# Two of four units of a layer's last step: transposed in blocks on VectorE and moved through DRAM instead of on TensorE

## The reference

```python
for layer in (1, 2):
    h = layer_norm(x)                                  # scale and offset
    q, k, v = h @ wq + bq, ctx @ wk + bk, ctx @ wv + bv  # 16 heads of 128
    k, v = append(k, bias_k), append(v, bias_v)        # one learned key and value
    w = softmax(q @ k.T / sqrt(128))
    x = x + (w @ v) @ wo + bo
h = layer_norm(x)
x = x + gelu(h @ w_fc1 + b_fc1) @ w_fc2 + b_fc2
```

## Time and profile before

| | us |
|---|---|
| median of 3 runs | 495.98 |
| lowest, highest run | 494.83, 497.55 |
| profiled execution, its own time | 495.7 |
| its span in the trace | 493.9 |
| layer 0's last step, first score | 205.08 |
| layer 1's last step, first score | 434.04 |

### The profile page before, as it was taken

How to read it: one execution, slowest core, us unless ns; L and a number is a source line. 1 busy time by engine, 2 the same in 40 slices (tenths; PEclk the granted TensorE clock), 3 DMA queues, 4 the chain that set the end, 5 groups by cost and what they waited for, 6 DMA issues and landing times.

```text
span 493.9 us, 11020 instructions
## 1 busy us (share of the span) xinstructions
PE 487.9 (99%) x3216; PEld 442.2 (90%) x3216; DVE 389.8 (79%) x910; ACT 331.3 (67%) x728; POOL 413.9 (84%) x385
## 2 busy tenths in 40 slices
PE   8999999999999999999999999999999999999997
PEld 6789888999999898999988889989989989999997
DVE  4888878878877878857789878778788888766796
ACT  4777767666766866665486777758666677768542
POOL 4977989989898998996597989989989898999561
PEclk9999999999999999999999999999999999999999
DMA  7536777756567676612115786676766566650011
GB/s 240 182 107 199 247 238 211 209 188 193 176 208 195 210 215 191 198 40 66 42 44 172 237 252 183 209 205 195 229 188 196 186 200 185 194 169 1 15 32 42
DMA packets 53159, 82.56 MB, mean 167 GB/s; under 512 B 5904, under 2 KB 33936, under 8 KB 53136
## 3 DMA queue, kind: packets, MB, share of 16 engines
q1 hardware_dynamic: 53136, 82.28, 54.8%
HBM read 53.42 MB, written 28.84 MB: 167 GB/s over the span
## 4 chain that ended last, share of the span: by engine, by line
PE 90%; DMA 3%; DVE 3%; POOL 1%; SPq 1%; issue 1%; ACT 1%; ACTq 0%; DVEq 0%; POOLq 0%
PE ring L1224 67%; PE ps_ctx L1224 10%; PE acc L1224 10%; DMA spill<-blocks 1%; PE ring L1270 1%; DMA all_cols<-cols_in 1%; DMA wf_lo<-spill 1%; SPq L287 1%; DVE pT_lo L922 0%; PE ring L1307 0%; DVE h_lo L1003 0%; POOL rstd L412 0%; ACT q_hi L598 0%; DVE blocks L900 0%; POOL wf_lo L370 0%
## 5 line engine op out<-in xcount | busy, mean ns | idle before, releaser
L937 DVE TENSOR_REDUCE row_max<-ring 128x1 f32<-128x512 f32 x112 | 76.1, 688 | 27.6 <-PE ring L1224 27.3
L661 ACT ACTIVATE probs<-ring,shift 128x512 f32<-128x512 f32 x112 | 76.5, 684 | 18.7 <-DVE shift L942 18.6
L432 POOL TENSOR_TENSOR v_lo<-v_sum,v_hi 128x512 fp32r<-128x512 f32 x64 | 83.0, 1299 | 3.0 <-ACT v_hi L611 3.0
L900 DVE STREAM_TRANSPOSE blocks<-probs 128x512 f32<-128x512 f32 x108 | 70.1, 687 | 5.6 <-POOL probs L439 5.4
L439 POOL TENSOR_SCALAR probs<-probs,inv 128x512 f32<-128x512 f32 x80 | 55.5, 701 | 20.3 <-DVE inv L950 20.2
L444 POOL TENSOR_TENSOR pT_lo<-wf_lo,pT_hi 128x1024 fp32r<-128x1024 f32 x28 | 67.1, 2418 | 0.0
L1224 PE MATMUL ring<-pT_lo,v_hi 128*128 128x256 f32 x208 | 58.5, 281 | 0.2 <-DVE pT_lo L922 0.2
L1224 PE MATMUL ring<-pT_hi,v_lo 128*128 128x256 f32 x208 | 58.0, 279 | 0.0
L1224 PE MATMUL ring<-pT_hi,v_hi 128*128 128x256 f32 x208 | 58.0, 279 | 0.0
L593 ACT ACTIVATE k_hi<-ring,cols 128x512 fp32r<-128x512 f32 x57 | 37.7, 689 | 30.1 <-PE ring L1224 30.0
L1224 PE MATMUL ring<-wv_lo,cT_hi 128*128 128x256 f32 x200 | 55.9, 279 | 0.0
(11 more groups left out here) (215 smaller groups left out, 1634.6 us busy)
## 6 DMA issues: line engine op xcount, KB each, us to landing
spill<-blocks SPq DMA_DIRECT2D x54, 512.0 KB, 2.9
wf_lo<-spill SPq DMA_DIRECT2D x112, 128.0 KB, 3.3
wf_hi<-spill SPq DMA_DIRECT2D x104, 128.0 KB, 3.1
wk_raw<-wk_in SPq DMA_DIRECT2D x17, 256.0 KB, 2.7
wq_raw<-wq_in SPq DMA_DIRECT2D x17, 256.0 KB, 3.7
wv_raw<-wv_in SPq DMA_DIRECT2D x16, 256.0 KB, 3.9
vrows<-vrows_in SPq DMA_DIRECT2D x16, 256.0 KB, 4.1
wo_raw<-wo_in SPq DMA_DIRECT2D x16, 256.0 KB, 2.7
```

The costliest lines, as they stand in the source:

```text
L432: pool.tensor_tensor(v_lo[:, 2 * m:2 * m + 2, :], v_sum[:, m % 2, :].rearrange("p (t c) -> p t c", c=PW), v_hi[:, 2 * m:2 * m + 2, :].bitc ...
L661: act.activation(probs[:, u, q, :], ring[S_BANKS[where][QTB * u + q]][:], ACT.Exp, bias=shift[:, u, q:q + 1], scale=SCALE, accum_out=row_s ...
L900: last = dve.transpose(blocks[:, u % 2, :, :, q, :].rearrange("p g c b -> p c g b"), probs[:, u, q, :].rearrange("p (c g b) -> p c g b", g ...
L937: dve.reduce_max(row_max[:, u, q:q + 1], ring[S_BANKS[where][QTB * u + q]][:], AX_X).then_inc(max_done, 1)
```

## The change

In `last_step` the units 0 and 1 go the way of the steady steps: `transpose_blocks` on VectorE, `write_blocks` and `read_blocks` on SP, `round_moved` on ScalarE, `moved_rest` on VectorE. Only units 2 and 3 are transposed on TensorE: `transpose_own` 0 to 3 are now what 4 to 7 were (`NT` is 4 instead of 8). The orders of all engines in `last_step` are changed with it. Since the steady machinery now runs in every step for units 0 and 1, the semaphore counts lose their `- layer` (`pair - layer` becomes `pair`), and SP adds by hand, for units 2 and 3 of a last step, what their moves would have added.

Cut to its core (left out: the renamed counts in the helpers):

```diff
-NT = NU * 2
+NT = 4
-PT_BANKS = [3, 1, 4, 0, 3, 0, 5, 0]
+PT_BANKS = [3, 0, 5, 0]
...
@@ SP @@
-            def last_step(pair, final=False):
+            def last_step(pair, layer, final=False):
+                sp.wait_ge(wo_split, pair)
+                load_wo(pair)
+                for u in range(2):
+                    write_blocks(pair, layer, u, False)
+                for u in range(2):
+                    read_blocks(pair, layer, u, False)
+                for u in range(2, NU):
+
+                    sp.wait_ge(landed[u], QB * LOAD * pair)
+                    sp.sem_inc(blocks_ready, 1)
+                    sp.sem_inc(landed[u], QB * LOAD)
+                    sp.sem_inc(spilled[u], LOAD)
                 if not final:
                     sp.wait_ge(wk_split, pair + 2)
                     load_wk(pair + 2)
-                sp.wait_ge(wo_split, pair)
-                load_wo(pair)
-                if not final:
                     sp.wait_ge(wo_split, pair + 1)
                     load_wo(pair + 1)
...
@@ GpSimd, last_step @@
                 split_wo(pair - 1)
-                residual(layer, 0)
-                normalise(pair, 0, [0])
+                normalise(pair, 0, [0, 1])
+                normalise(pair, 1, [1])
                 moved_rest(pair - 1, layer, 2)
                 value_rest(pair, 0)
                 moved_rest(pair - 1, layer, 3)
-                normalise(pair, 0, [1])
-                normalise(pair, 1, [1])
+                normalise(pair, 2, [0, 1])
                 value_rest(pair, 1)
                 pool.wait_ge(k_filled, NK * (pair + 1))
                 split_wk(pair + 1)
-                normalise(pair, 2, [0, 1])
-                residual(layer, 1)
+                residual(layer, 0)
+                value_rest(pair, 2)
                 pool.wait_ge(outputs_done, layer + 1)
                 split_wo(pair)
-                value_rest(pair, 2)
                 value_rest(pair, 3)
+                residual(layer, 1)
                 inverse_deviation(layer + 1, 0)
...
@@ ScalarE @@
             def exponential(pair, u, q, where, layer, first=False):
-                if not first:
-                    act.wait_ge(blocks_ready, NU * (pair - 1 - layer) + u + 1)
+                if not first or layer > 0:
+                    act.wait_ge(blocks_ready, NU * (pair - 1) + u + 1)
...
@@ ScalarE, last_step @@
                 exponential(pair, 1, 1, "last", layer)
                 round_v(pair, 0, layer)
+                normalise(pair, 1, [0])
                 round_moved(pair - 1, layer, 3)
                 round_o(pair - 1, 1, "last")
                 exponential(pair, 2, 0, "last", layer)
                 round_v(pair, 1, layer)
                 exponential(pair, 2, 1, "last", layer)
-                normalise(pair, 1, [0])
                 round_o(pair - 1, 2, "last")
                 exponential(pair, 3, 0, "last", layer)
-                round_o(pair - 1, 3, "last")
-                round_own(pair, layer, 0)
-                round_own(pair, layer, 1)
-                round_own(pair, layer, 2)
                 exponential(pair, 3, 1, "last", layer)
                 round_v(pair, 2, layer)
-                round_own(pair, layer, 3)
-                normalise(pair, 3, [0])
+                normalise(pair, 3, [0, 1])
+                round_o(pair - 1, 3, "last")
+                round_moved(pair, layer, 0)
+                if final:
+                    act.activation(table_load[:], dim_cols[:, 0:1], ACT.Gelu)
+                round_moved(pair, layer, 1)
+                round_v(pair, 3, layer)
                 if not final:
                     round_k(pair + 1, 0, "last")
-                else:
-                    act.activation(table_load[:], dim_cols[:, 0:1], ACT.Gelu)
-                round_v(pair, 3, layer)
-                normalise(pair, 3, [1])
                 round_o(pair, 0, "own")
                 round_o(pair, 1, "own")
-                round_own(pair, layer, 4)
-                round_own(pair, layer, 5)
-                round_own(pair, layer, 6)
-                round_own(pair, layer, 7)
+                for j in range(NT):
+                    round_own(pair, layer, j)
...
@@ VectorE, last_step @@
                 maximum(pair, 1, 0, "last")
-                split_o(pair - 1, 0, "last")
                 shifts(pair, 1, 0)
                 maximum(pair, 1, 1, "last")
+                shifts(pair, 1, 1)
+                inverse_sums(pair, 0)
+                split_o(pair - 1, 0, "last")
                 dve.wait_ge(wv_split, pair + 1)
                 sum_v(pair, 0, "last")
-                inverse_sums(pair, 0)
-                shifts(pair, 1, 1)
+                inverse_sums(pair, 1)
+                transpose_blocks(pair, layer, 0)
+                transpose_blocks(pair, layer, 1)
                 maximum(pair, 2, 0, "last")
+                shifts(pair, 2, 0)
                 sum_v(pair, 1, "last")
-                shifts(pair, 2, 0)
                 maximum(pair, 2, 1, "last")
                 shifts(pair, 2, 1)
-                inverse_sums(pair, 1)
                 split_o(pair - 1, 1, "last")
                 maximum(pair, 3, 0, "last")
                 shifts(pair, 3, 0)
                 maximum(pair, 3, 1, "last")
                 shifts(pair, 3, 1)
+                inverse_sums(pair, 2)
                 split_o(pair - 1, 2, "last")
                 sum_v(pair, 2, "last")
-                split_own(pair, layer, 0)
-                split_own(pair, layer, 1)
-                inverse_sums(pair, 2)
+                inverse_sums(pair, 3)
                 split_o(pair - 1, 3, "last")
-                split_own(pair, layer, 2)
-                inverse_sums(pair, 3)
+                moved_rest(pair, layer, 0)
                 sum_v(pair, 3, "last")
-                split_own(pair, layer, 3)
+                moved_rest(pair, layer, 1)
                 split_o(pair, 0, "own")
...
@@ TensorE, last_step @@
                 pe.wait_ge(v_summed, NV * pair + 2)
                 context(2, "last")
                 unit_output(0)
                 pe.wait_ge(o_split, NU * (pair - 1) + 2)
                 project_v(2, "last")
-                pe.wait_ge(pT_split[3], done)
+                pe.wait_ge(pT_split[3], pair)
                 pe.wait_ge(exp_done, NS * pair + 5)
                 context(3, "last")
+                unit_output(1)
                 pe.wait_ge(exp_done, NS * pair + 6)
-                transpose_own(0)
-                pe.wait_ge(p_ready_pool, NORMS_POOL * pair + 2)
-                pe.wait_ge(v_summed, NV * pair + 3)
-                transpose_own(1)
-                pe.wait_ge(p_ready_act, NORMS_ACT * pair + 1)
-                pe.wait_ge(exp_done, NS * pair + 7)
-                transpose_own(2)
-                pe.wait_ge(p_ready_pool, NORMS_POOL * pair + 3)
-                transpose_own(3)
-                unit_output(1)
-                pe.wait_ge(own_split, own + 1)
                 project_v(3, "last")
+                pe.wait_ge(o_split, NU * (pair - 1) + 3)
                 unit_output(2)
                 if not final:
                     pe.wait_ge(wk_split, pair + 2)
                     pe.wait_ge(o_split, NU * pair)
                     project_k(0, "last")
                 pe.wait_ge(o_split, NU * pair)
                 unit_output(3).then_inc(outputs_done, 1)
                 pe.wait_ge(v_split, NV * pair + 2)
-                pe.wait_ge(own_split, own + 3)
+                pe.wait_ge(pT_split[0], pair + 1)
+                pe.wait_ge(exp_done, NS * pair + 7)
                 context(0, "own")
-                pe.wait_ge(own_split, own + 4)
+                pe.wait_ge(pT_split[1], pair + 1)
+                pe.wait_ge(v_summed, NV * pair + 3)
                 context(1, "own")
                 pe.wait_ge(p_ready_pool, NORMS_POOL * pair + 4)
-                transpose_own(4)
+                pe.wait_ge(v_summed, NV * (pair + 1))
+                transpose_own(0)
                 pe.wait_ge(p_ready_pool, NORMS_POOL * (pair + 1))
-                transpose_own(5)
+                transpose_own(1)
```

More of the change, by code:

```diff
@@ L280, in read_blocks @@
             def read_blocks(pair, layer, u, first):
-                done = pair - layer
                 if not first or layer > 0:
-                    hold(pT_split[u], done)
-                hold(spilled[u], LOAD * (done + 1))
+                    hold(pT_split[u], pair)
+                hold(spilled[u], LOAD * (pair + 1))
                 for g in range(QB):
@@ L1150, in last_step @@
                 split_o(pair, 1, "own")
-                split_own(pair, layer, 4)
-                split_own(pair, layer, 5)
+                split_own(pair, layer, 0)
+                split_own(pair, layer, 1)
                 new_x(layer, 0)
@@ L1158, in last_step @@
                     moments(layer + 1, 0)
-                split_own(pair, layer, 6)
-                split_own(pair, layer, 7)
+                split_own(pair, layer, 2)
```

(10 more changed lines are left out.)

61 lines of the change are left out of this document (30 added, 31 removed).

## The result

The changed kernel takes 502.06 us (median of six runs, 500.55 to 502.56), the kernel before 495.81 on the same chip (494.83 to 497.55): a ratio of 1.012, 95% interval 1.0099 to 1.014. It is slower, as forecast, but by 6.3 us where 2.8 were forecast, and it lies 1.1 us above the top of the range. The profiled execution took 502.05, its span is 500.2 against 493.9.

What follows compares the result with a forecast made beforehand. TensorE, busy 99% of the span, was taken to bound the kernel. Removed 3.5 us, added 2.15 in layer 0 and 4.15 in layer 1, net 2.8 us slower: 498.8 us against a median of 495.98, range 495.0 to 501.0.

Steps and rivals of the forecast that it cites:

- The removed 1.75 us per layer: Four of eight transpose_own leave TensorE in each last step: 1.75 us per layer, 3.5 us in two layers.
- The first wait: Each last step: context(2, "last") waits for sum_v(1), queued on VectorE behind transposes that wait for ScalarE; 1.58 us lost.
- a wait put into TensorE's queue costs its whole time: Last step, TensorE always busy at full clock: each wait costs its length, plus 0.1 us for the first matmul.
- one layer's times can be carried to the other: Last steps: the same point lies 228.96 us apart, so layer 0's times were carried to layer 1.
- The second wait: Behind context(3): project_k(0) 0.25 us late in layer 0; own contexts 0 and 1 1.4 and 2.4 late in layer 1.
- The route through DRAM, costed at nothing,: Last steps: moved blocks of units 0 and 1 land before ScalarE wants them at median transfer times; cost 0.
- Rival 3: Moved blocks land late from DRAM, at the largest landings: 5.8 us slower, 501.8 us; chance 0.12.
- Rival 1: Waits in the last steps are hidden and only the transposes go: 3.5 us gained, 492.5 us; chance 0.11.
- rival 2: No first wait at context(2), only the second behind context(3): 495.6 us, no change; chance 0.15.
- 2.15 for layer 0: Time added in layer 0's last step: 1.68 + 0.35 + 0.1 us.

Runs made afterwards that it cites:

- e6: Changed kernel with e1's and e2's moves, ScalarE's round_o(3) and round_moved ahead of normalise(3), and GpSimd's weight splits earlier in the last steps; 495.74 us.
- e1: Changed kernel with ScalarE's normalise(1, [0]) moved ahead of round_v(0) in the last step; 498.03 us.
- e4: Changed kernel with seven matmuls of zeros added ahead of the waits of context(2) in both last steps; 500.28 us.
- b1: Kernel before with only sum_v(1) moved back in VectorE's queue, behind the first maximum of unit 3, in the last steps; 502.35 us.
- e2: Changed kernel with VectorE's sum_v(1) moved between the two transpose_blocks of the last step; 498.89 us.
- e3: Changed kernel with ScalarE's round_o(3) moved first behind the last exponential, and both round_moved ahead of normalise(3) and the gelu table; 501.37 us.
- e8: e6 with sum_v(1) ahead of both block transposes, round_moved(0) right behind round_o(3), and the table load between the two round_moved; 495.34 us.
- e5: Changed kernel with 14 instructions that only count added at TensorE's start; 501.08 us.
- e7: e6 with the 14 counting instructions of e5 at TensorE's start; 495.46 us.
- e9: e8 with 28 counting instructions added at TensorE's start; 497.74 us.
- e10: e8 with seven tiny products of zeros added where TensorE waits in layer 0's prologue, its wait for the first value sum moved ahead of them; 494.98 us.
- b2: Kernel before with 14 instructions that only count added at TensorE's start; 496.94 us.

## Why the prediction came out as it did

**The removed 1.75 us per layer** are right: 1.69 in layer 0 once nothing waits (e6).

**The first wait** is right in place, releaser and chain (e1), and low in size: `context(2)` came 1.98 late in layer 0, 1.72 in layer 1, against 1.58. Of the 0.40 too little in layer 0, 0.33 lies in the start of the second transposes, 215.32 against 214.99. ScalarE's `normalise` had ended at 214.87; in layer 1 the transposes followed it by 0.09, here by 0.45. What took the difference is not settled.

**Two steps failed. The first is "a wait put into TensorE's queue costs its whole time"**, taken to mean no more than that time, with 0.1 us for the first matmul after it. A wait of 1.9 to 2.0 us cost more when behind it the granted clock fell to 0.57: the stretch to `context(3)` took 1.65 us longer in layer 0 of the profiled execution. e1 and e4 take the idle time away, by order and by other work, and the clock stays at 1.00; b1 puts the wait into the kernel before, and the clock falls. It does not fall in each execution: the six runs of the changed kernel show a mean clock of 0.997 in three, 502.37 us in the mean, and of 1.000 in three, 501.40. So the clock is not the whole miss: without its fall the change still costs 5.6 us, twice the forecast. The Trainium skill, TensorE: Matmul & The Clock Gate, "HAM oscillation — how this bites in real kernels", tells of waits between groups of matmuls after which the next ones run at the lower clock. The trace agrees, with 0.57 behind 1.89 us of idle time, and this belonged among the rivals.

**The second is "one layer's times can be carried to the other".** Layer 1's last step has the standstill of 1.41 us, which neither layer 0 nor the kernel before shows there, and which no wait in the program explains. The changed kernel and every variant of it with TensorE's instructions where they lay (e1, e2, e3, e6, e8) have it, with 1.29 to 1.43; every variant that moved them (e4, e5, e7, e9, e10) does not. The six come to this step at 431.9 to 436.2 us, the five at 433.1 to 437.9, so the moment does not decide it; by these eleven profiles the place of the instructions does. How it does so is not shown. A transfer on the instruction queue lies close to the moment at which TensorE comes to this step, while the DMA engines are taken by moved blocks (DMA queues of the changed kernel, 435.5 to 436.0: packets, MB, share):

```profile
q1 hardware_dynamic: 128, 0.11, 82.6%
q8 instruction: 1, 0.02, 15.3%
```

This queue divides the kernels in the same way. The six with the standstill have no transfer on it from 258 to 431 us, then one within 0.3 us of the step's first score and another some 4 to 5 us later. The eight without (before, b1 and b2 among them) have one between 273 and 280 us, then one 0.4 to 1.0 us after the first score. That TensorE waits for such a transfer is argued from this, not shown: no row ties it to TensorE.

The losses of the loop steps are 0 in the changed kernel, e1, e6 and e8, 0.6 in before, 0.7 to 2.0 in b1, b2, e4, e5, e7, e9 and e10, and 1.3 and 0.6 in e2 and e3. Layer 1's loop loses 0.4 to 2.0 in the eight kernels without the standstill and nothing in the six with it, so moving the instructions gave back little. The large ones are waits for moved blocks: ScalarE's `round_moved` stands 2.3 to 2.9 us for their landing in a first loop step of e2, e4, b1, e9 and e10, and at most 1.7 in the changed kernel, e1, e6 and e8. In e4, first ScalarE, then TensorE behind it:

```profile
291.13 1.06 ACT L634 ACTIVATE pT_hi<-wf_hi 128x1024 fp32r<-128x1024 f32 x1 [2.86 <-DMA wf_hi<-spill]
294.03 1.06 ACT L634 ACTIVATE pT_hi<-wf_hi 128x1024 fp32r<-128x1024 f32 x1 [1.84 <-DMA wf_hi<-spill]
```

```profile
296.02 0.39 PE L1225 MATMUL acc<-wo_lo,o_hi 128*128 128x256 f32 x1 [1.49 <-DVE o_lo L931]
```

Why these landings are late is open. The 0.4 that the table above gives back between layer 1's first query product and its last step is before's own loss in its loop steps.

**The second wait** is right: own context 0 is 1.35 late by layer 1's own clock (4.87 less 2.11 and 1.41) against 1.4, own context 1 2.8 against 2.4, with `pT_lo` as releaser at 462.96 and the table load between. For own context 0 the row names no releaser ("issue"), but unit 0's `pT_lo` ended 0.10 before it (458.74 and 1.24 long, against 460.08). From the table load to the next `round_moved` it took 1.40, as the earlier trace rows had it, 1.28 of it the load. The Trainium skill, ScalarE: Activation LUTs, "What ACT_TABLE_LOAD costs", has 2.66 us, about half of it the load and half a drain. The load's 1.28 agrees; the drain does not show here. In layer 0 `project_k(0)` waits 0.3, as forecast.

**The route through DRAM, costed at nothing,** is right for the changed kernel, as the row at 227.05 shows. Rival 3 lies nearest to the measured time, and its mechanism is not what happened; it turns up in layer 1 once the queues are in order (1.60 in e6). Rival 1 fell with the first wait, rival 2 with both.

The sum for the profiled execution, then: 2.8 forecast, 1.55 for the slow stretch (1.65 less the 0.1 forecast there), 1.41 for the standstill, 0.4 each for the late transposes and for own context 1, less the 0.4 of before's loop steps: 6.2 of 6.3. (The forecast's 2.15 for layer 0 is 2.13 by its own terms, which changes nothing here.) For the runs without the clock's fall the same sum gives 4.6 of 5.6; none of them was profiled, and 1.0 stays open.

## What to carry to other kernels

Where TensorE sets the time, a wait in its queue is not only its own length: look at the granted clock of the stretch behind it, and count matmuls there, since busy time does not show a slow clock. When work moves to another engine, read that engine's queue for what now stands behind each of its waits; here one ScalarE instruction moved up by one place was worth 4.0 of the 6.3 us lost. And free time on an engine is worth what the next late thing allows: five waits had to be taken away (unit 2's context, two own contexts, two on GpSimd's splits) before TensorE's saving was seen in one layer, and in the other it was not.

## What was not expected of the hardware

- The granted clock fell to 0.57 and 0.62 in the stretch behind idle times of 1.89 and 2.04 us, in some executions of the same kernel and not in others, with DMA at 0.90 and at 0.01; it did not fall behind 1.53 in layer 1 of the changed kernel, nor behind 1.03 in e2, nor behind the second wait of 2.04 in b1.
- TensorE stood still 1.41 us inside a product, with no wait of the program there, and instructions added hundreds of microseconds earlier in the program took that away.
- Fourteen instructions that only count held back TensorE's first matmul from 1.31 to 2.92 us, twenty-eight to 5.08.
